# The offset of the first layer norm: from a negated mean on VectorE and a product on GpSimd to one more VectorE instruction behind the inverse root

## Chip, cores and metric

One core of one Trainium2 chip runs the kernel. The metric is the device time of one execution in microseconds (us); lower is better. Engines are written PE (TensorE), DVE (VectorE), ACT (ScalarE), POOL (GpSimd) and SP (SyncE, which issues DMAs here).

## What is computed

Two graph layers on 128 graphs of 128 nodes with 128 features, each with a residual and a layer norm. With this adjacency (0 or 1, ones on the diagonal) the 39 relations of the first layer that need values from 2 to 40 are empty, and so are three of the four relations of the second.

```python
def _layernorm(x, axis=-1, eps=1e-05):
    m = jnp.mean(x, axis=axis, keepdims=True)
    v = jnp.var(x, axis=axis, keepdims=True)
    return (x - m) / jnp.sqrt(v + eps)
...
h = x @ W.T
g = h @ Wg.T
vals = (h[:, :, None, :] + b) * jax.nn.sigmoid(g[:, :, None, :] + bg)
...
x = _layernorm(x + relu(adj_t @ vals))            # first layer, in short
x = _layernorm(x + (adj == 1) @ x @ weight + bias)  # second layer, in short
```

## The kernel before

The 128 graphs are taken in 32 groups of 4 (`GROUPS`, `GB`), a tile being 128 partitions (nodes) by 512 (4 graphs by 128 features), all fp32. The group number is q, and each engine has its own program, written as a loop over iterations t in which it works on several groups at different stages. Nothing but that written order and semaphores orders the work.

In iteration t, PE projects group t (`hg_ps`, L379), sums the neighbours of group t-1 (`loop_ps`, L391), multiplies the messages of group t-5 by their weights (`y_ps`, L430) and gathers the messages of group t-3 (`msg_ps`, L409). ACT makes the gate of group t (L524), seeds the next bank (L515), copies messages (L534), writes normalised output (L551) and looks at the adjacency (L560).

DVE does in iteration t, in this order: the second sum `z_sb` of group t-5 (L753) and its two halves of statistics (L757), the gated values of group t (L727), the first sum `s_sb` of group t-1 (L735) and its statistics (L742). Between these stand the nine steps of one inverse root per iteration, the chain (`inverse_root`, L665, L668, L671, L676, L679, L682, L685, L688, L691), on tiles of 128 by 8: four graphs of the first norm and four of the second. Every step reads the one before it and waits for it by the semaphore `chain_done`. The ninth writes `rstd`. In iterations 2 to 4, before the first `z_sb` exists, all nine steps run in one piece ahead of the values (L727); from iteration 5 on they are woven between the large instructions, and the ninth stands right before the next `z_sb`.

The first norm is x1 = s * rstd + nmr with nmr = -mean * rstd. Its means are read with the statistics: `negative_means` writes `mean_neg` (L710, 128 by 4), called between the third and fourth step of the chain. POOL waits for `chain_done` and `mean_done`, multiplies to `nmr` (L320, 128 by 4), waits for that product, and makes x1 in four instructions, one a graph (L328). It then issues one adjacency DMA (L303 or L310). PE's messages of that group wait for `x1_done`, and DVE's own `z_sb` and the reuse of the rings do too. The last group's product is made by DVE (`last_norm1`, L790), and its x1 is shared by POOL, DVE and ACT.

Of the kernel before, what the change touches and what calls it, by code (L numbers as in the profile page):

```python
# [59 lines left out]
def build(nc, x, x_t, adj, adj_t, w_in, w_loop_t, wg_loop_t, gate_bias, w_msg, msg_bias,  # L60
          w_rel_t, wg_rel_t, b_rel, bg_rel, w_msgs, rel_ids, identity, out):
    with ExitStack() as ctx:
        def sb(name, shape, dt):
            return ctx.enter_context(nc.sbuf_tensor(name, shape, dt))
# [20 lines left out]
        stats = sb("stats", [P, STATS_RING, 4, 6], F32)  # L85
        rstd = sb("rstd", [P, RSTD_RING, 2, GB], F32)
        nmr = sb("nmr", [P, 2, GB], F32)
        mean_neg = sb("mean_neg", [P, 2, GB], F32)
        tiny = sb("tiny", [P, 2, 6, 2 * GB], F32)
        last_stats = sb("last_stats", [P, 2, 4, 6], F32)  # L90
        last_rstd = sb("last_rstd", [P, 2, 2 * GB], F32)
# [71 lines left out]
        bn2_done = sem("bn2_done")  # L163
        chain_done = [sem(f"chain_done{j}") for j in range(2)]
        last_done = [sem(f"last_done{j}") for j in range(2)]
        mean_done = sem("mean_done")
        nmr_done = sem("nmr_done")
        last_nmr = sem("last_nmr")
        last_bn = sem("last_bn")
        x1_act = sem("x1_act")  # L170
        x1_dve = sem("x1_dve")
# [124 lines left out]
        @block.gpsimd  # L296
        def _(pool):
            def load_adj(k):
                if 0 <= k < PAIRS:
                    spot = k % ADJ_RING  # L300
                    await_count(pool, loop_done, 2 * (k - ADJ_RING) + 2)
                    await_count(pool, seen_done, 2 * (k - ADJ_RING) + 2)
                    pool.dma_start(adj_sb[:, 2 * spot:2 * spot + 2, :].rearrange("p g n -> p (g n)"), adj[k])\  # L303
                        .then_inc(adj_in[spot], 16)

            def load_adjt(k):
                if 0 <= k < PAIRS:
                    spot = k % ADJ_RING
                    await_count(pool, msg_done, 2 * (k - ADJ_RING) + 2)
                    pool.dma_start(adjt_sb[:, 2 * spot:2 * spot + 2, :].rearrange("p g n -> p (g n)"), adj_t[k])\  # L310
                        .then_inc(adjt_in[spot], 16)

            def norm1(q):
                if exists(q):
                    t = q + NORM1_LAG
                    pool.wait_ge(chain_done[t % 2], chain_end(t))
                    r, n = rstd[:, t % RSTD_RING, 0, :], nmr[:, t % 2, :]
                    if q < GROUPS - 1:
                        pool.wait_ge(mean_done, q + 1)
                        nc.gpsimd.tensor_tensor(n, mean_neg[:, t % 2, :], r, ALU.mult).then_inc(nmr_done, 1)  # L320
                        pool.wait_ge(nmr_done, q + 1)
                    else:
                        pool.wait_ge(last_nmr, 1)

                    await_count(pool, msg_done, q - X1_RING + 1)
                    await_count(pool, z_done, q - X1_RING + 1)
                    for b in range(GB) if q < GROUPS - 1 else (2,):
                        last = nc.gpsimd.tensor_scalar(  # L328
                            x1[:, q % X1_RING, batch(b)], s_sb[:, q % S_RING, batch(b)],
                            r[:, b:b + 1], n[:, b:b + 1], ALU.mult, ALU.add)  # L330
                    last.then_inc(x1_done, 1)


            pool.wait_ge(fold_in, 16 * 2)
            load_adj(0)
            load_adj(1)
            load_adjt(0)
            load_adj(2)
            load_adjt(1)
            for t in range(GROUPS + NORM1_LAG):  # L340
                norm1(t - NORM1_LAG)
                if t % 2 == 0:
                    load_adj(t // 2 + 3)
                else:
                    load_adjt(t // 2 + 2)

            def general_pair(pair):
                pool.dma_start(adj_sb[:, 0:2, :], adj[bass.ds(pair, 1)].rearrange("o p (g n) -> p (o g) n", g=2))\
                    .then_inc(gadj_in, 16)
                pool.dma_start(adjt_sb[:, 0:2, :], adj_t[bass.ds(pair, 1)].rearrange("o p (g n) -> p (o g) n", g=2))\  # L350
                    .then_inc(gadj_in, 16)
                pool.wait_ge(gout_ready, pair * 2 + 2)

            general(pool, general_pair)
# [145 lines left out]
        def _(act):  # L500
# [76 lines left out]
            copy_messages(GROUPS - 3)  # L577
            norm2(GROUPS - 6, every)
            copy_messages(GROUPS - 2)
            act.wait_ge(last_nmr, 1)  # L580
            t = GROUPS - 1 + NORM1_LAG
            nc.scalar.activation(x1[:, (GROUPS - 1) % X1_RING, batch(3)], s_sb[:, (GROUPS - 1) % S_RING, batch(3)],
                                 ACT.Identity, bias=nmr[:, t % 2, 3:4],
# [43 lines left out]
        def _(dve):  # L627
# [32 lines left out]
                dve.wait_ge(w1_mid, 4)  # L660
                tt(w1[:, :], b1_mid[:, :], aux_ps[:, P:2 * P], ALU.subtract).then_inc(w1_mid, 2)

            def inverse_root(m2, r, done, before, work, aside=None):
                var, y0, y1, yy, a, w = (work[:, i, :] for i in range(6))
                ts(var, m2, 1.0 / P, EPS, ALU.mult, ALU.add).then_inc(done, 1)  # L665
                yield
                dve.wait_ge(done, before + 1)
                ts(y0.bitcast(I32), var.bitcast(I32), -0.5, GUESS, ALU.mult, ALU.add).then_inc(done, 1)  # L668
                yield
                dve.wait_ge(done, before + 2)  # L670
                tt(yy, y0, y0, ALU.mult).then_inc(done, 1)  # L671
                yield
                if aside is not None:
                    aside()
                dve.wait_ge(done, before + 3)
                tt(a, yy, var, ALU.mult).then_inc(done, 1)  # L676
                yield
                dve.wait_ge(done, before + 4)
                stt(w, a, CUBIC1, a, ALU.add, ALU.mult).then_inc(done, 1)  # L679
                yield  # L680
                dve.wait_ge(done, before + 5)
                stt(y1, w, CUBIC0, y0, ALU.add, ALU.mult).then_inc(done, 1)  # L682
                yield
                dve.wait_ge(done, before + 6)
                tt(yy, y1, y1, ALU.mult).then_inc(done, 1)  # L685
                yield
                dve.wait_ge(done, before + 7)
                stt(w, yy, -0.5, var, ALU.mult, ALU.mult).then_inc(done, 1)  # L688
                yield
                dve.wait_ge(done, before + 8)  # L690
                stt(r, w, 1.5, y1, ALU.add, ALU.mult).then_inc(done, 1)  # L691

            def chain(t):

                if FIRST_CHAIN <= t <= LAST_CHAIN:
                    await_count(dve, bn1_done, t - NORM1_LAG + 1)
                    await_count(dve, bn2_done, t - STAT2_LAG + 1)

                    await_count(dve, x1_done, t - RSTD_RING - NORM1_LAG + 1)
                    await_count(dve, out_done, t - RSTD_RING - STAT2_LAG + 1)  # L700
                    before = chain_end(t) - CHAIN_OPS
                    await_count(dve, chain_done[t % 2], before)
                    m2 = stats[:, t % STATS_RING, :, :].rearrange("p c (i k) -> p (c i) k", k=3)[:, :, 2]
                    r = rstd[:, t % RSTD_RING, :, :].rearrange("p l b -> p (l b)")

                    def negative_means():

                        await_count(dve, x1_done, t - 2 - NORM1_LAG + 1)
                        means = stats[:, t % STATS_RING, 0:2, :].rearrange("p c (i k) -> p (c i) k", k=3)[:, :, 1]
                        ts(mean_neg[:, t % 2, :], means, -1.0, None, ALU.mult).then_inc(mean_done, 1)  # L710

                    yield from inverse_root(m2, r, chain_done[t % 2], before, tiny[:, t % 2, :, :], negative_means)

            def last_chain(k):

# [67 lines left out]
            def last_norm1(q):  # L783
                t = q + NORM1_LAG
                r, n = rstd[:, t % RSTD_RING, 0, :], nmr[:, t % 2, :]
                dve.wait_ge(chain_done[t % 2], chain_end(t))

                dve.wait_ge(x1_done, q - 1)
                dve.wait_ge(mean_done, q + 1)
                tt(n, mean_neg[:, t % 2, :], r, ALU.mult).then_inc(last_nmr, 1)  # L790
                dve.wait_ge(last_nmr, 1)

                dve.wait_ge(msg_done, q - X1_RING + 1)
                dve.wait_ge(z_done, q - X1_RING + 1)
                for b in range(2):
                    last = ts(x1[:, q % X1_RING, batch(b)], s_sb[:, q % S_RING, batch(b)], r[:, b:b + 1], n[:, b:b + 1],
                              ALU.mult, ALU.add)
                last.then_inc(x1_dve, 1)
# [7 lines left out]
            for t in range(GROUPS + 1):  # L806
# [6 lines left out]
                if exists(t - Z_LAG):  # L813
                    second_sum(t - Z_LAG)
                    step(1)
                    second_stats(t - Z_LAG, 0)
                    step(1)
                    second_stats(t - Z_LAG, 1)
                    step(2)
                else:  # L820
                    step(CHAIN_OPS)
                if exists(t):
                    values(t)
                if t == 1:
# [4 lines left out]
                if exists(t - LOOP_LAG):  # L829
# [2 lines left out]
                    first_stats(t - LOOP_LAG, 0)  # L832
                    step(1)
                    first_stats(t - LOOP_LAG, 1)
                step(CHAIN_OPS)
            for _ in chain(LAST_CHAIN):
                pass
            last_norm1(GROUPS - 1)
# [136 lines left out]
```

## Time and profile before

| what | value |
|---|---|
| time, median of 3 runs | 169.39 us (169.31 to 169.51) |
| the profiled execution: its time, and its span | 168.68 us, 166.9 us |
| TensorE clock granted, mean | 0.985 |
| busy, share of the span | PE 91%, DVE 88%, ACT 75%, POOL 47% |
| chain that ended last | PE 78%, DMA 8%, DVE 7% |

The span runs from the first to the last instruction; the execution's time is 1.78 us longer than its span. Busy time counts an instruction from its start to its end. On DVE consecutive instructions overlap in the trace by 0.06 to 0.09 us, so what one costs is read from the distance between starts and not from its duration.

### The profile page before, as it was taken

What the parts mean: (1) busy time and instruction counts of PE and PEld (TensorE: products, weight loads), DVE (VectorE), ACT (ScalarE), POOL (GpSimd) and SP (SyncE); (2) the same over time, 40 slices, a digit from 0 to 9 for tenths busy, and PEclk for the clock granted to TensorE, in tenths of its full rate; (3) what the DMA queues carried; (4) which work ended last, traced back from release to release, by engine and by line L of the source; (5) the groups of instructions that cost most, each with busy time, mean ns of one, the idle gap of its engine ahead of it and who ended that gap; (6) DMA issues with size and microseconds to landing.
All of it is one profiled execution on the core that took longest, in us unless ns stands there. A gap on an engine that the chain in (4) does not pass through costs nothing.

```text
span 166.9 us, 3913 instructions
## 1 busy us (share of the span) xinstructions
PE 151.6 (91%) x1072; PEld 140.4 (84%) x1072; DVE 146.7 (88%) x583; ACT 126.0 (75%) x287; POOL 78.6 (47%) x192
## 2 busy tenths in 40 slices
PE   6864899999999999999999999999999999998920
PEld 2553689999999999999999999999999999997910
DVE  1225999999999999999999999999999999999771
ACT  3266455679888888888888889998888888844661
POOL 2700366155555555565555555555554544446000
PEclk9999999999999999999999999999999999999985
DMA  4999999965999999999999899999995341131133
GB/s 137 342 389 394 397 401 403 308 196 189 298 302 306 310 304 274 280 312 301 268 305 329 272 277 333 325 310 298 253 324 212 85 166 63 65 130 63 64 125 138
DMA packets 19465, 42.76 MB, mean 256 GB/s; under 512 B 2160, under 2 KB 3056, under 8 KB 19440
## 3 DMA queue, kind: packets, MB, share of 16 engines
q1 hardware_dynamic: 13968, 25.24, 44.0%
q0 software_dynamic: 4608, 16.78, 33.2%
q10 hardware_dynamic: 864, 0.46, 0.9%
q8 instruction: 10, 0.16, 0.4%
q14 instruction: 15, 0.12, 0.3%
HBM read 34.08 MB, written 8.39 MB: 254 GB/s over the span
## 4 chain that ended last, share of the span: by engine, by line
PE 78%; DMA 8%; DVE 7%; issue 3%; ACT 1%; ACTq 0%; DVEq 0%
PE hg_ps L379 28%; PE msg_ps L409 16%; PE y_ps L430 15%; PE loop_ps L391 15%; DMA b<-msg_bias_dram 5%; DMA gate_b<-gate_bias_dram 2%; PE hg_ps L430 2%; PE hg_ps L426 2%; DVE s_sb L735 2%; DVE stats L742 1%; PE y_ps L426 1%; PE hg_ps L409 1%; ACT out_sb L551 1%; DVE z_sb L753 0%; DVE tiny L679 0%
## 5 line engine op out<-in xcount | busy, mean ns | idle before, releaser
L379 PE MATMUL hg_ps<-w_gate,xt_sb 128*128 128x256 f32 x256 | 60.8, 380 | 2.6 <-ACT hg_ps L515 2.5
L328 POOL TENSOR_SCALAR x<-s_sb,rstd,nmr 128x128 f32<-128x128 f32 x125 | 54.7, 446 | 3.7 <-DVE rstd L691 0.4
L379 PEld LDWEIGHTS hg_ps<-w_gate,xt_sb 128*128 128x128 f32 x256 | 46.2, 190 | 8.5 <-issue 3.0
L320 POOL TENSOR_TENSOR nmr<-mean_neg,rstd 128x4 f32<-128x4 f32 x31 | 6.0, 194 | 68.8 <-DVE rstd L691 68.8
L551 ACT ACTIVATE out_sb<-z_sb,rstd 128x128 f32<-128x128 f32 x112 | 38.0, 391 | 0.2 <-DVE rstd L691 0.2
L391 PEld LDWEIGHTS loop_ps<-vals,adj_sb 128*128 128x128 f32 x256 | 33.3, 191 | 5.2 <-issue 3.8
L391 PE MATMUL loop_ps<-vals,adj_sb 128*128 128x128 f32 x256 | 34.0, 276 | 2.6 <-DVE s_sb L735 2.6
L524 ACT ACTIVATE gate<-hg_ps 128x512 f32<-128x512 f32 x32 | 19.1, 597 | 22.2 <-PE hg_ps L379 22.1
L515 ACT ACTIVATE hg_ps<-gate_b 128x1024 f32<-128x1024 f32 (+1 forms) x32 | 32.3, 1010 | 1.0 <-DMA gate_b<-gate_bias_dram 1.0
L409 PE MATMUL msg_ps<-adjt_sb,x 128*128 128x128 f32 x248 | 33.0, 276 | 0.0
L430 PE MATMUL y_ps<-w,msg_t 128*128 128x128 f32 x232 | 30.6, 275 | 0.0
L409 PEld LDWEIGHTS msg_ps<-adjt_sb,x 128*128 128x128 f32 x248 | 30.2, 192 | 0.2 <-issue 0.2
L430 PEld LDWEIGHTS y_ps<-w,msg_t 128*128 128x128 f32 x232 | 28.2, 192 | 0.0
L727 DVE TENSOR_TENSOR vals<-hg_ps,gate 128x512 f32<-128x512 f32 x32 | 22.0, 688 | 6.4 <-ACT gate L524 5.7
L742 DVE BATCH_NORM_STATS2 stats<-s_sb 128x6 f32<-128x256 f32 x64 | 26.5, 426 | 0.3
L757 DVE BATCH_NORM_STATS2 stats<-z_sb 128x6 f32<-128x256 f32 x56 | 23.7, 427 | 0.0
L560 ACT ACTIVATE seen<-adj_sb,half 128x512 bf16<-128x512 f32 x32 | 22.7, 710 | 1.3 <-DMA adj_sb<-adj_dram 1.3
L534 ACT ACTIVATE msg_t<-msg_ps 128x512 f32<-128x512 f32 x31 | 18.0, 581 | 6.6 <-PE msg_ps L409 6.6
L735 DVE SCALAR_TENSOR_TENSOR s_sb<-loop_ps,x_sb 128x512 f32<-128x512 f32 x32 | 21.8, 682 | 0.0
L753 DVE TENSOR_TENSOR z_sb<-y_ps,x 128x512 f32<-128x512 f32 x28 | 19.1, 682 | 0.0
L303 POOL DMA_DIRECT2D adj_sb<-adj_dram x16 | 9.6, 598 | 2.8 <-DMA wg_t<-wg_loop_t_dram 2.8
L310 POOL DMA_DIRECT2D adjt_sb<-adj_t_dram x16 | 9.5, 591 | 0.0
(66 smaller groups left out, 104.9 us busy)
## 6 DMA issues: line engine op xcount, KB each, us to landing
xt_sb<-x_t_dram SPq DMA_DIRECT2D x32, 256.0 KB, 4.9
x_sb<-x_dram SPq DMA_DIRECT2D x32, 256.0 KB, 5.0
adj_sb<-adj_dram POOLq DMA_DIRECT2D x16, 512.0 KB, 5.5
adjt_sb<-adj_t_dram POOLq DMA_DIRECT2D x16, 512.0 KB, 5.2
out<-out_sb SPq DMA_DIRECT2D x32, 256.0 KB, 4.1
gate_b<-gate_bias_dram ACTq DMA_DIRECT2D x1, 128.0 KB, 3.4
w_loop<-w_loop_dram ACTq DMA_DIRECT2D x1, 64.0 KB, 2.0
wg_t<-wg_loop_t_dram SPq DMA_DIRECT2D x1, 64.0 KB, 2.2
```

What stands on the lines that cost most here:

```text
L328: last = nc.gpsimd.tensor_scalar(x1[:, q % X1_RING, batch(b)], s_sb[:, q % S_RING, batch(b)], r[:, b:b + 1], n[:, b:b + 1], ALU.mult, ALU.add)
L379: last = nc.tensor.matmul(hg_ps[:, q % 2, b, :], xt_sb[:, q % XT_RING, batch(b)], w_gate[:, :], start=False, stop=True, skip_group_check=True)
L391: last = nc.tensor.matmul(loop_ps[:, batch(b)], adj_sb[:, spot, batch(b)], vals[:, q % 2, batch(b)], start=True, stop=True)
L409: last = nc.tensor.matmul(msg_of(q)[:, batch(b)], x1[:, q % X1_RING, batch(b)], adjt_sb[:, spot, batch(b)], start=True, stop=True)
L430: last = nc.tensor.matmul(y_of(q)[:, batch(b)], msg_t[:, q % 2, batch(b)], w1[:, :], start=q < LAST, stop=True, skip_group_check=q >= LAST)
L515: nc.scalar.activation(hg_ps[:, q % 2, 0:graphs, :], gate_b[:, None, :].broadcast_to([P, graphs, 2 * P]), ACT.Copy).then_inc(seeded, 1)
L551: last = nc.scalar.activation(out_sb[:, q % OUT_RING, batch(b)], src, ACT.Copy, scale=r)
L560: nc.scalar.activation(seen[:, :], adj_sb[:, 2 * spot + q % 2, :], ACT.Square, bias=half[:, 0:1], accum_out=seen_sum[:, q:q + 1]).then_inc ...
L727: tt(vals[:, q % 2, :].rearrange("p (b n) -> p b n", b=GB), hg_ps[:, q % 2, :, 0:P], gate[:, q % 2, :].rearrange("p (b n) -> p b n", b=GB) ...
L735: stt(s_sb[:, q % S_RING, :], loop_ps[:, :], 0.0, x_sb[:, q % X_RING, :], ALU.max, ALU.add)\
L742: got = nc.vector.bn_stats(stats[:, (q + NORM1_LAG) % STATS_RING, p, :], s_sb[:, q % S_RING, 2 * p * P:2 * (p + 1) * P].rearrange("p (i n) ...
L757: got = nc.vector.bn_stats(stats[:, (q + STAT2_LAG) % STATS_RING, 2 + p, :], z_sb[:, q % Z_RING, 2 * p * P:2 * (p + 1) * P].rearrange("p ( ...
```

## The change

The negated means are gone, with their tile, the product on POOL and the one in `last_norm1`. Behind the ninth step DVE waits for it and writes `nmr` itself in one instruction, (mean * -1) * rstd, from the statistics and `rstd`; the semaphore `nmr_done` now carries it to POOL, ACT and DVE. The places at which the program lets "all remaining" steps run now take ten.

```diff
             def norm1(q):
                 if exists(q):
                     t = q + NORM1_LAG
-                    pool.wait_ge(chain_done[t % 2], chain_end(t))
                     r, n = rstd[:, t % RSTD_RING, 0, :], nmr[:, t % 2, :]
-                    if q < GROUPS - 1:
-                        pool.wait_ge(mean_done, q + 1)
-                        nc.gpsimd.tensor_tensor(n, mean_neg[:, t % 2, :], r, ALU.mult).then_inc(nmr_done, 1)
-                        pool.wait_ge(nmr_done, q + 1)
-                    else:
-                        pool.wait_ge(last_nmr, 1)
+
+                    pool.wait_ge(nmr_done, q + 1)
...
-                    def negative_means():
-
-                        await_count(dve, x1_done, t - 2 - NORM1_LAG + 1)
-                        means = stats[:, t % STATS_RING, 0:2, :].rearrange("p c (i k) -> p (c i) k", k=3)[:, :, 1]
-                        ts(mean_neg[:, t % 2, :], means, -1.0, None, ALU.mult).then_inc(mean_done, 1)
-
-                    yield from inverse_root(m2, r, chain_done[t % 2], before, tiny[:, t % 2, :, :], negative_means)
+                    yield from inverse_root(m2, r, chain_done[t % 2], before, tiny[:, t % 2, :, :])
+                    yield
+                    dve.wait_ge(chain_done[t % 2], before + CHAIN_OPS)
+
+                    await_count(dve, x1_done, t - 2 - NORM1_LAG + 1)
+                    means = stats[:, t % STATS_RING, 0:2, :].rearrange("p c (i k) -> p (c i) k", k=3)[:, :, 1]
+                    stt(nmr[:, t % 2, :], means, -1.0, rstd[:, t % RSTD_RING, 0, :], ALU.mult, ALU.mult)\
+                        .then_inc(nmr_done, 1)
...
             def last_norm1(q):
                 t = q + NORM1_LAG
                 r, n = rstd[:, t % RSTD_RING, 0, :], nmr[:, t % 2, :]
-                dve.wait_ge(chain_done[t % 2], chain_end(t))
-
-                dve.wait_ge(x1_done, q - 1)
-                dve.wait_ge(mean_done, q + 1)
-                tt(n, mean_neg[:, t % 2, :], r, ALU.mult).then_inc(last_nmr, 1)
-                dve.wait_ge(last_nmr, 1)
+                dve.wait_ge(nmr_done, q + 1)
```

On DVE the first place is the first chain, iteration 2, which ends ahead of `vals`. Before:

```order
L671 TENSOR_TENSOR tiny<-tiny 128x8
L710 TENSOR_SCALAR mean_neg<-stats 128x4
L676 TENSOR_TENSOR tiny<-tiny 128x8
L679 SCALAR_TENSOR_TENSOR tiny<-tiny 128x8
L682 SCALAR_TENSOR_TENSOR tiny<-tiny 128x8
L685 TENSOR_TENSOR tiny<-tiny 128x8
L688 SCALAR_TENSOR_TENSOR tiny<-tiny 128x8
L691 SCALAR_TENSOR_TENSOR rstd<-tiny 128x8
L727 TENSOR_TENSOR vals<-hg_ps,gate 128x512
```

And the same place on DVE with the change (its line numbers are those of the changed file, 8 to 10 lower):

```order
L663 TENSOR_TENSOR tiny<-tiny 128x8
L666 TENSOR_TENSOR tiny<-tiny 128x8
L669 SCALAR_TENSOR_TENSOR tiny<-tiny 128x8
L672 SCALAR_TENSOR_TENSOR tiny<-tiny 128x8
L675 TENSOR_TENSOR tiny<-tiny 128x8
L678 SCALAR_TENSOR_TENSOR tiny<-tiny 128x8
L681 SCALAR_TENSOR_TENSOR rstd<-tiny 128x8
L702 SCALAR_TENSOR_TENSOR nmr<-stats,rstd 128x4
L718 TENSOR_TENSOR vals<-hg_ps,gate 128x512
```

The filler between two dependent steps has gone, and a dependent instruction stands at the end, ahead of the values. On DVE the second place is the turn from one iteration to the next once the chain is woven in (from iteration 5). Before:

```order
L742 BN_STATS stats<-s_sb 128x6
L691 SCALAR_TENSOR_TENSOR rstd<-tiny 128x8
L753 TENSOR_TENSOR z_sb<-y_ps,x 128x512
L665 TENSOR_SCALAR tiny<-stats 128x8
L757 BN_STATS stats<-z_sb 128x6
L668 TENSOR_SCALAR tiny<-tiny 128x8
L757 BN_STATS stats<-z_sb 128x6
L671 TENSOR_TENSOR tiny<-tiny 128x8
L710 TENSOR_SCALAR mean_neg<-stats 128x4
L676 TENSOR_TENSOR tiny<-tiny 128x8
L727 TENSOR_TENSOR vals<-hg_ps,gate 128x512
```

With the change, on DVE at the same place:

```order
L733 BN_STATS stats<-s_sb 128x6
L681 SCALAR_TENSOR_TENSOR rstd<-tiny 128x8
L702 SCALAR_TENSOR_TENSOR nmr<-stats,rstd 128x4
L744 TENSOR_TENSOR z_sb<-y_ps,x 128x512
L657 TENSOR_SCALAR tiny<-stats 128x8
L748 BN_STATS stats<-z_sb 128x6
L660 TENSOR_SCALAR tiny<-tiny 128x8
L748 BN_STATS stats<-z_sb 128x6
L663 TENSOR_TENSOR tiny<-tiny 128x8
L666 TENSOR_TENSOR tiny<-tiny 128x8
L718 TENSOR_TENSOR vals<-hg_ps,gate 128x512
```

The new instruction stands between the ninth step and `z_sb`, with nothing between it and the step that it reads. On POOL one iteration before, with its waits in brackets:

```order
L320 TENSOR_TENSOR nmr<-mean_neg,rstd 128x4 [waits mean_done,chain_done0]
L328 TENSOR_SCALAR x<-s_sb,rstd,nmr 128x128 [waits z_done,msg_done,nmr_done]
L328 TENSOR_SCALAR x<-s_sb,rstd,nmr 128x128 x3
L303 DMA adj_sb<-adj_dram 128x1024 [waits seen_done,loop_done]
```

And on POOL with the change:

```order
L320 TENSOR_SCALAR x<-s_sb,rstd,nmr 128x128 [waits z_done,msg_done,nmr_done]
L320 TENSOR_SCALAR x<-s_sb,rstd,nmr 128x128 x3
L300 DMA adj_sb<-adj_dram 128x1024 [waits seen_done,loop_done]
```

POOL's first instruction of a group is now x1 itself (the changed file's L320 is the old L328).

## Rows read from the trace of the kernel before

**Rows 1.** The chain that ended last, shares of the span by engine.

```profile
PE 78%; DMA 8%; DVE 7%; issue 3%; ACT 1%; ACTq 0%; DVEq 0%
```

**Rows 2.** 58 to 145 us: length; busy PE, PEld, DVE, ACT, POOL; clock; DMA.

```profile
58.00:145.00 87.00, 87.00 (x632) 82.87 (x631) 85.56 (x338) 76.75 (x180) 47.51 (x116) 1.00 0.83 258
```

**Rows 3.** Timeline of one iteration, 81 to 85.5 us: start us, us, what.

```profile
81.01 0.68 DVE L753 TENSOR_TENSOR z_sb<-y_ps,x 128x512 f32<-128x512 f32 x1
81.18 0.19 POOL L320 TENSOR_TENSOR nmr<-mean_neg,rstd 128x4 f32<-128x4 f32 x1 [1.82 <-DVE rstd L691]
...
81.48 1.73 POOL L328 TENSOR_SCALAR x<-s_sb,rstd,nmr 128x128 f32<-128x128 f32 x4
81.61 0.15 DVE L665 TENSOR_SCALAR tiny<-stats 128x8 f32<-128x8 f32 x1
...
82.07 0.31 DVE L668 TENSOR_SCALAR tiny<-tiny 128x8 int32<-128x8 int32 x1
...
82.41 0.60 ACT L524 ACTIVATE gate<-hg_ps 128x512 f32<-128x512 f32 x1 [0.52 <-PE hg_ps L379]
82.63 0.17 DVE L671 TENSOR_TENSOR tiny<-tiny 128x8 f32<-128x8 f32 x1
82.72 0.15 DVE L710 TENSOR_SCALAR mean_neg<-stats 128x4 f32<-128x4 f32 x1
82.83 0.21 DVE L676 TENSOR_TENSOR tiny<-tiny 128x8 f32<-128x8 f32 x1
...
83.03 0.69 DVE L727 TENSOR_TENSOR vals<-hg_ps,gate 128x512 f32<-128x512 f32 x1
...
83.99 1.06 PE L409 MATMUL msg_ps<-adjt_sb,x 128*128 128x128 f32 x8
84.32 0.15 DVE L682 SCALAR_TENSOR_TENSOR tiny<-tiny 128x8 f32<-128x8 f32 x1
...
84.50 0.17 DVE L685 TENSOR_TENSOR tiny<-tiny 128x8 f32<-128x8 f32 x1
...
85.34 0.15 DVE L691 SCALAR_TENSOR_TENSOR rstd<-tiny 128x8 f32<-128x8 f32 x1
85.41 0.69 DVE L753 TENSOR_TENSOR z_sb<-y_ps,x 128x512 f32<-128x512 f32 x1
```

**Rows 4.** Timelines of DVE and of POOL in an early iteration.

```profile
33.10 0.68 DVE L753 TENSOR_TENSOR z_sb<-y_ps,x 128x512 f32<-128x512 f32 x1
...
34.17 0.15 DVE L668 TENSOR_SCALAR tiny<-tiny 128x8 int32<-128x8 int32 x1
...
34.66 0.28 DVE L710 TENSOR_SCALAR mean_neg<-stats 128x4 f32<-128x4 f32 x1
...
37.28 0.68 DVE L753 TENSOR_TENSOR z_sb<-y_ps,x 128x512 f32<-128x512 f32 x1
...
33.58 1.76 POOL L328 TENSOR_SCALAR x<-s_sb,rstd,nmr 128x128 f32<-128x128 f32 x4
```

**Rows 5.** Timeline of PE at the start of the loop.

```profile
20.56 1.13 PE L391 MATMUL loop_ps<-vals,adj_sb 128*128 128x128 f32 x8 [0.74 <-DVE s_sb L735]
...
35.44 0.79 PE L409 MATMUL msg_ps<-adjt_sb,x 128*128 128x128 f32 x5
```

**Rows 6.** Timeline of the end of the loop, 147 to 154 us.

```profile
147.03 0.15 DVE L691 SCALAR_TENSOR_TENSOR rstd<-tiny 128x8 f32<-128x8 f32 x1
...
150.90 0.15 DVE L691 SCALAR_TENSOR_TENSOR rstd<-tiny 128x8 f32<-128x8 f32 x1
...
151.44 1.84 POOL L328 TENSOR_SCALAR x<-s_sb,rstd,nmr 128x128 f32<-128x128 f32 x4
...
151.63 0.31 DVE L676 TENSOR_TENSOR tiny<-tiny 128x8 f32<-128x8 f32 x1
...
152.90 0.40 DVE L691 SCALAR_TENSOR_TENSOR rstd<-tiny 128x8 f32<-128x8 f32 x1
...
153.39 1.13 PE L409 MATMUL hg_ps<-adjt_sb,x 128*128 128x128 f32 x8 [0.76 <-issue]
```

More of the change, by code:

```diff
@@ L87, in build @@
         nmr = sb("nmr", [P, 2, GB], F32)
-        mean_neg = sb("mean_neg", [P, 2, GB], F32)
         tiny = sb("tiny", [P, 2, 6, 2 * GB], F32)
@@ L165, in build @@
         last_done = [sem(f"last_done{j}") for j in range(2)]
-        mean_done = sem("mean_done")
         nmr_done = sem("nmr_done")
-        last_nmr = sem("last_nmr")
         last_bn = sem("last_bn")
@@ L579, in _ @@
             copy_messages(GROUPS - 2)
-            act.wait_ge(last_nmr, 1)
+            act.wait_ge(nmr_done, GROUPS)
             t = GROUPS - 1 + NORM1_LAG
@@ L661, in message_weight_end, with inverse_root @@
                 tt(w1[:, :], b1_mid[:, :], aux_ps[:, P:2 * P], ALU.subtract).then_inc(w1_mid, 2)
-            def inverse_root(m2, r, done, before, work, aside=None):
+            def inverse_root(m2, r, done, before, work):
                 var, y0, y1, yy, a, w = (work[:, i, :] for i in range(6))
@@ L672, in inverse_root @@
                 yield
-                if aside is not None:
-                    aside()
                 dve.wait_ge(done, before + 3)
@@ L820, in _ @@
                 else:
-                    step(CHAIN_OPS)
+                    step(CHAIN_OPS + 1)
                 if exists(t):
@@ L834, in _ @@
                     first_stats(t - LOOP_LAG, 1)
-                step(CHAIN_OPS)
+                step(CHAIN_OPS + 1)
             for _ in chain(LAST_CHAIN):
```

## The prediction

> **What bounds the kernel now.** I read the chain that ended last first: PE holds 78% of it [rows 1]. The busy time by stretch then shows a PE without a gap from 58 to 145 us (87.00 of 87.00 us), but also a DVE that is busy for 85.56 of them [rows 2]. So PE sets the pace, and DVE runs right beside it; the question is how much room DVE has, and only the timeline of one iteration tells.
>
> One iteration takes 85.41 - 81.01 = 4.40 us, z_sb to z_sb [rows 3]. DVE has one real wait in it: the gate ends at 82.41 + 0.60 = 83.01, and `vals` starts at 83.03. Without that wait `vals` would follow L676 some 0.09 us before that one's end (83.04), at 82.95. DVE's room is 0.08 us an iteration, its own pace 4.32. In the early iteration of [rows 4] it ran at 37.28 - 33.10 = 4.18. The difference has a cause that matters below: L668 took 0.31 us in the one and 0.15 in the other.
>
> **A small instruction beside POOL.** POOL's x1 is four instructions of 0.43 to 0.44 us each. L668 at 82.07 starts 0.16 us into the second (81.48 + 0.43 = 81.91), takes 0.31 and ends 0.47 behind that one's start. At 34.17 it is 0.15 us into the second (33.58 + 0.44) and takes 0.15. L710 at 34.66 starts 0.20 into the third and takes 0.28; L710 at 82.72 starts 0.37 into one and takes 0.15; L676 at 151.63 starts 0.19 into the first (151.44), takes 0.31 and ends 0.50 behind its start [rows 3, 4, 6]. So a small DVE instruction that starts between about 0.16 and 0.3 us into a POOL instruction is held until that ends, and one that starts earlier or later goes through.
>
> **The change part by part.**
>
> Removed on DVE: L710. L671 starts at 82.63 and L676, which waits for it, at 82.83: 0.20. L682 to L685, dependent too and with nothing between, is 0.18 [rows 3]. L710 stood in the shadow of that wait, so its removal returns 0, at most 0.02. Removed on POOL: L320 with its wait. From the start of L691 to x1 it is 81.48 - 81.01 + 0.07 = 0.54 (L691 starts 0.07 ahead of z_sb, 85.34 to 85.41).
>
> Added on DVE: `nmr` behind L691, which it reads. Before, L691 to the next instruction was 0.07 [rows 3]. Now L691 to `nmr` is a dependent distance, 0.18 to 0.20 (I take 0.19), and `nmr` to the next 0.08: 0.27, so +0.20 us an iteration. The trace has no such instruction of 128 by 4 with three operands; the dependent steps of 128 by 8 at 0.17 are the nearest rows. Bounds: +0.01, if it had a plain place in line (0.08), and +0.20 as said. The dependence is written in the code, so I take +0.20. POOL gets `nmr` at 0.19 + 0.17 and starts 0.10 later (L691's end, 81.01 - 0.07 + 0.15 = 81.09, to L320 at 81.18 was 0.09): x1 starts 0.46 to 0.47 behind L691, 0.07 earlier than before.
>
> The start. In iterations 2 to 4 the chain stands in one piece ahead of `vals` and `s_sb`, and PE waits for `s_sb` (0.74 us at 20.56 [rows 5]). Each of the three chains puts DVE back by 0.20, hence 0.60 by iteration 5. There POOL's x1 for group 3 ends at 33.58 + 1.76 = 35.34 [rows 4], and PE's messages start at 35.44, 0.1 behind it [rows 5]: this hand-over decides. Shift of PE from here: 0.60 - 0.07 = **+0.53 us**. There is no cover for it, since PE has no gap behind it.
>
> The even part. Where do DVE's small steps fall against POOL now? Counting from the start of z_sb, POOL's first x1 starts at 0.46 - 0.27 = 0.19 and its fourth at 0.19 + 1.30 = 1.49. L668 (at 1.06) starts 0.01 into the third, so its stretch of 0.16 goes. L671 comes at 1.62 - 0.16 = 1.46, and L676 at 1.66: 0.17 to 0.18 into the fourth. By the rows above it is held until 0.47 to 0.50 behind that one's start, 1.96 to 1.99, and `vals` could start at 1.87 to 1.90. From `vals` to the next z_sb it is 85.41 - 83.03 = 2.38, and +0.20 for `nmr`. DVE's own pace becomes 4.45 to 4.48 us; with 0.02 on the distances, 4.42 to 4.48. I take **4.45**, which is above PE's 4.40. Then DVE no longer catches up after the start and sets the pace: x1 arrives later each time, and PE waits at its messages. In the even part x1 was ready at 81.48 + 1.73 = 83.21 and wanted at 83.99 [rows 3], but the start uses this slack up.
>
> The end. PE waits 0.76 us at 153.39 for x1 of group 30, which POOL ended at 151.44 + 1.84 = 153.28 [rows 6]; behind it PE runs without DVE's help until the last statistics. So the shift of that x1 is the shift of the whole. From L691 of iteration 5 (33.10 - 0.06 = 33.04) to that of iteration 32 (150.90) it was 117.86 us. Now it is 26 x 4.45, and a last period without `vals` of about 4.0 (150.90 - 147.03 = 3.87 before, +0.20 for `nmr`, -0.16 for L668, +0.10 for L676): 119.7, or +1.84.
>
> Sum: 0.53 + 1.84 = **+2.4 us**, 171.1 against this execution's 168.68. The median of runs is 0.71 above that execution, so 169.39 + 2.4 = **171.8 us**. With 4.42 or 4.48 in place of 4.45 it is 0.8 less or more: 171.0 to 172.6.
>
> **A rule that makes it worse.** The trace lets an instruction through that starts up to 0.15 us into a POOL instruction: L665 at 81.61 is 0.13 into the first and takes 0.15 [rows 3]. If such an early start were held as well, L668, now 0.01 into the third, would be held to 0.19 + 0.87 + 0.47 = 1.53 in place of 1.21: L671 would come at 1.78, L676 at 1.98 when POOL is through, `vals` at 2.06, and the pace would be 2.06 + 2.38 + 0.20 = 4.64. The Trainium skill (SBUF — State Buffer, Who interferes with whom) has this rule: VectorE and GpSimd lock a shared port pair for a whole instruction, and the later one is fully blocked. By that rule the trace agrees for starts from 0.16 us on and disagrees for L665.
>
> **The rivals.**
>
> (a) PE stays the bound. If L676 slips through, `vals` could start at 1.66 + 0.09 = 1.75, and the pace is 1.75 + 2.38 + 0.20 = 4.33, under 4.40. Then only the start remains, and the end (+0.20 for `nmr`, -0.16 for L668, -0.07 on POOL) is -0.03: +0.5 us, 169.9. It decides at L676's start, 0.15 or 0.16 into the fourth; I have 0.17 to 0.18. For it speaks that the distance to the edge is 0.02 us; against it, that L691 at 152.90 took 0.40 beside a fourth instruction [rows 6], and that L676 at 82.83 took 0.21 when hardly 0.06 into one.
>
> (b) The early start is held too, pace 4.64: 0.53 + 117.86 replaced by 26 x 4.64 + 4.3 = 124.9, so +7.6: 177.0. Against it speaks L665.
>
> (c) Not slower. `nmr` takes a place without a wait, at +0.01 in place of +0.20: then the start costs 0.03 and gives 0.07 on POOL, and the last period loses L668's 0.16 and POOL's 0.07, in all about -0.25 us: 169.1. This needs the dependent distance to fall under about 0.09 us; nothing in the trace does, all are 0.18 or more.
>
> **How the numbers follow.** DVE sets the pace (4.42 to 4.48): 0.65. (a) 0.22. (b) 0.04. (c) 0.04. The remaining 0.05 lies between the main case and (a), a pace near 4.40 that works the lag off slowly. A change of this kernel can be told from none at about 0.2%, 0.34 us. The likeliest is 171.8 with its own range of 171.0 to 172.6. The range that holds 8 in 10 reaches to (a) and leaves (b) and (c) out: 169.8 to 172.7. Slower holds the main case, (b), what lies between, and most of (a) (+0.5 against 0.34): 0.85; same the rest of (a) and part of (c): 0.11; faster 0.04.
>
> **What the changed profile would show.** In every iteration `nmr` starts 0.19 us behind the ninth step, and the next instruction 0.08 behind `nmr`; x1 starts on POOL 0.46 behind the ninth step. PE's messages at 35.44 come near 35.97. In the even part z_sb to z_sb is 4.45 and not 4.40, the fourth step takes about 0.3 us, L668 0.15, `vals` starts clear of the gate's end, and PE shows small waits at the messages. The prediction is wrong if the fourth step takes 0.15 to 0.21 us and the period is 4.40: then (a) holds.

## The result, and the profile after

The changed kernel takes 171.37 us (median of 4 runs, 170.90 to 172.08) beside 169.45 us for the kernel before (169.31 to 169.56): the ratio is 1.0116, with a 95% interval of 1.0091 to 1.0142. It is 1.9 us slower; 171.8 was forecast, and 171.0 to 172.6 as the likeliest case's own range. Between the two profiled executions (168.68 and 171.13 us) the difference is 2.45 us.

Three lines of the changed kernel's page, and its busy time by stretch from 58 to 145 us (columns as in [rows 2]):

```profile
span 169.3 us, 3878 instructions
...
DVE 54%; issue 27%; DMA 8%; PE 6%; DVEq 1%; ACT 1%; ACTq 0%
...
L666 DVE TENSOR_TENSOR tiny<-tiny 128x8 f32<-128x8 f32 x34 | 7.5, 219 | 1.2
```

```profile
58.00:145.00 87.00, 86.96 (x628) 82.72 (x627) 84.68 (x333) 76.11 (x177) 42.24 (x94) 1.00 0.83 263
```

The chain that ended last has gone from PE (78% in [rows 1]) to DVE, with 54%, and PE's share is 6%. "Issue" (27%) is time between the DVE instructions of that chain for which the profile shows no releaser. The busy times do not tell this at all: PE is busy for 86.96 of 87.00 us as before, and DVE, which now sets the pace, is busy for less than before (84.68 against 85.56 us), because the second step is no longer held and the fourth step and `nmr` stand behind short idle times, 0.04 and 0.03 us (84.69 to 84.73 and 82.91 to 82.94 below). L666, the old L676, is the fourth step of the chain.

One iteration of the changed kernel, timeline from 82.7 to 87.5 us:

```profile
82.76 0.15 DVE L681 SCALAR_TENSOR_TENSOR rstd<-tiny 128x8 f32<-128x8 f32 x1
...
82.94 0.16 DVE L702 SCALAR_TENSOR_TENSOR nmr<-stats,rstd 128x4 f32<-128x4 f32 x1
...
83.05 0.69 DVE L744 TENSOR_TENSOR z_sb<-y_ps,x 128x512 f32<-128x512 f32 x1
...
83.22 1.73 POOL L320 TENSOR_SCALAR x<-s_sb,rstd,nmr 128x128 f32<-128x128 f32 x4 [2.16 <-DVE nmr L702]
...
83.55 0.58 ACT L516 ACTIVATE gate<-hg_ps 128x512 f32<-128x512 f32 x1
...
84.13 0.15 DVE L660 TENSOR_SCALAR tiny<-tiny 128x8 int32<-128x8 int32 x1
...
84.53 0.16 DVE L663 TENSOR_TENSOR tiny<-tiny 128x8 f32<-128x8 f32 x1
84.73 0.23 DVE L666 TENSOR_TENSOR tiny<-tiny 128x8 f32<-128x8 f32 x1
84.89 0.68 DVE L718 TENSOR_TENSOR vals<-hg_ps,gate 128x512 f32<-128x512 f32 x1
...
87.48 0.69 DVE L744 TENSOR_TENSOR z_sb<-y_ps,x 128x512 f32<-128x512 f32 x1
```

z_sb to z_sb is 87.48 - 83.05 = 4.43 us (4.40 in [rows 3]). `vals` starts 0.76 us behind the gate's end (83.55 + 0.58 = 84.13) where before it waited for it. `nmr` starts 0.18 behind the ninth step, and z_sb 0.11 behind `nmr`, 0.29 in all where 0.07 was: +0.22. The second step (L660) takes 0.15 and is no longer held. The fourth step starts 0.22 us into POOL's fourth x1 instruction (84.51 to 84.95 in the trace), takes 0.23, and `vals` follows 0.16 behind its start and not 0.08.

Counted from z_sb's start, `vals` now starts at 1.84 us (84.89 - 83.05). In the kernel before it could start at 1.94 (82.95 by the prediction's estimate, less 81.01). So the insertion adds 0.22 us, and the steps ahead of `vals` give back about 0.1: the second step's hold is gone (-0.16), a new one stands at the fourth. That is how DVE's own pace comes from 4.32 to 4.43 us and not to 4.54.

Start and end of the changed kernel, from its timelines of PE, DVE and POOL:

```profile
16.16 0.68 DVE L726 SCALAR_TENSOR_TENSOR s_sb<-loop_ps,x_sb 128x512 f32<-128x512 f32 x1
...
21.00 1.13 PE L383 MATMUL loop_ps<-vals,adj_sb 128*128 128x128 f32 x8 [0.93 <-DVE s_sb L726]
...
21.45 0.59 POOL L300 DMA_DIRECT2D adj_sb<-adj_dram  x1
...
21.69 0.31 DVE L657 TENSOR_SCALAR tiny<-stats 128x8 f32<-128x8 f32 x1
...
25.36 1.13 PE L383 MATMUL loop_ps<-vals,adj_sb 128*128 128x128 f32 x8 [0.60 <-DVE s_sb L726]
...
33.98 0.15 DVE L681 SCALAR_TENSOR_TENSOR rstd<-tiny 128x8 f32<-128x8 f32 x1
...
34.44 1.73 POOL L320 TENSOR_SCALAR x<-s_sb,rstd,nmr 128x128 f32<-128x128 f32 x4 [4.04 <-DVE nmr L702]
...
36.27 0.91 PE L401 MATMUL msg_ps<-adjt_sb,x 128*128 128x128 f32 x6
...
118.83 0.69 DVE L744 TENSOR_TENSOR z_sb<-y_ps,x 128x512 f32<-128x512 f32 x1 [0.30 <-issue]
...
149.44 0.15 DVE L681 SCALAR_TENSOR_TENSOR rstd<-tiny 128x8 f32<-128x8 f32 x1
...
153.41 0.15 DVE L681 SCALAR_TENSOR_TENSOR rstd<-tiny 128x8 f32<-128x8 f32 x1
...
155.69 1.13 PE L401 MATMUL hg_ps<-adjt_sb,x 128*128 128x128 f32 x8 [0.43 <-issue]
```

PE waits longer for `s_sb` (0.93 us against 0.74 in [rows 5]), the messages of iteration 6 start at 36.27 (35.44), the ninth step of iteration 32 at 153.41 (150.90), and group 30's messages at 155.69 (153.39 in [rows 6]): 2.3 us later. Of that, 0.25 us is not the change's: the first s_sb of this execution starts at 16.16 and that of the kernel before at 15.91, behind a DMA of the message bias that ended at 14.61 and 14.35. The first s_sb of the kernel before, timeline of DVE:

```profile
15.91 0.68 DVE L735 SCALAR_TENSOR_TENSOR s_sb<-loop_ps,x_sb 128x512 f32<-128x512 f32 x1
```

### The profile page after: what moved, and what is told of

The parts are those of the page before. It is cut to its first block, busy times and chain, and to the rows that moved or that the text cites. A ratio compares the mean times of both kernels' runs of the same rounds, so it can differ in the third digit from the quotient of the medians.

```text
span 169.3 us, 3878 instructions
## 1 busy us (share of the span) xinstructions
PE 152.9 (90%) x1072; PEld 141.2 (83%) x1072; DVE 147.3 (87%) x582; ACT 125.8 (74%) x287; POOL 71.6 (42%) x161
## 4 chain that ended last, share of the span: by engine, by line
DVE 54%; issue 27%; DMA 8%; PE 6%; DVEq 1%; ACT 1%; ACTq 0%
DVE stats L748 11%; DVE s_sb L726 11%; DMA b<-msg_bias_dram 6%; DVE stats L733 5%; DVE tiny L657 3%; DVE vals L718 3%; DVE rstd L681 3%; DVE tiny L669 3%; DVE tiny L678 3%; DVE z_sb L744 2%; DMA gate_b<-gate_bias_dram 2%; DVE tiny L663 2%; DVE tiny L672 2%; PE hg_ps L422 2%; DVE tiny L660 2%
## 5 line engine op out<-in xcount | busy, mean ns | idle before, releaser
L320 POOL TENSOR_SCALAR x<-s_sb,rstd,nmr 128x128 f32<-128x128 f32 x125 | 54.3, 441 | 82.0 <-DVE nmr L702 82.0
L401 PE MATMUL msg_ps<-adjt_sb,x 128*128 128x128 f32 x248 | 33.5, 278 | 0.1
L516 ACT ACTIVATE gate<-hg_ps 128x512 f32<-128x512 f32 x32 | 18.6, 580 | 10.1 <-PE hg_ps L371 10.1
L666 DVE TENSOR_TENSOR tiny<-tiny 128x8 f32<-128x8 f32 x34 | 7.5, 219 | 1.2
```

The lines of the kernel that those rows point to most:

```text
L320: last = nc.gpsimd.tensor_scalar(x1[:, q % X1_RING, batch(b)], s_sb[:, q % S_RING, batch(b)], r[:, b:b + 1], n[:, b:b + 1], ALU.mult, ALU.add)
L401: last = nc.tensor.matmul(msg_of(q)[:, batch(b)], x1[:, q % X1_RING, batch(b)], adjt_sb[:, spot, batch(b)], start=True, stop=True)
```

## The experiments

They ran in three groups (E1 to E4, E5 to E8, E9 to E12), each on a chip of its own, the ratio each time to the kernel before on that chip (medians 168.7 to 168.9 us). There its runs spread over more than 1%, so the intervals are wider. Much of the spread lies ahead of the loop: in the profiled executions the first s_sb starts anywhere between 15.24 and 16.68 us. So where traces are compared below, times are counted from it. "The old way" is the negated mean on DVE and the product on POOL.

### Where it costs: the start and the loop apart

E1 is the kernel before with `nmr` on DVE in the first three chains alone; E2 is the changed kernel with the old way there, and E6 is E2 again, beside E5, the changed kernel again.

```diff
+OLD = 3
...
-                    pool.wait_ge(nmr_done, q + 1)
+                    if q < OLD:
+                        pool.wait_ge(chain_done[t % 2], chain_end(t))
+                        pool.wait_ge(mean_done, q + 1)
+                        nc.gpsimd.tensor_tensor(n, mean_neg[:, t % 2, :], r, ALU.mult).then_inc(nmr_old, 1)
+                        pool.wait_ge(nmr_old, q + 1)
+                    else:
+                        pool.wait_ge(nmr_done, q + 1 - OLD)
```

> The kernel before, with the new way (nmr on VectorE behind the ninth step) in the first three chains alone, iterations 2 to 4. Theory (two causes, start and pace): the three insertions put VectorE and so the x1 of group 3 back by 3 x 0.20 = 0.60 us, and from there the old loop runs at PE's 4.40 with VectorE catching up; total +0.6 us, 170.05, and PE's messages of iteration 6 start near 36.04 in place of 35.44. Rival (only the pace of the even part costs): no change, 169.4.

> The changed kernel, with the old way (negated means and a product on GpSimd) in the first three chains alone. Theory: VectorE's pace in the even part stays 4.43 us and sets the time from the first woven iteration on, but all of it begins 0.60 us earlier: 171.37 - 0.6 = 170.8. Rival (only the pace costs): 171.4, as the changed kernel.

> The changed kernel once more, on the same chip as the three beside it, as their base. Theory: 1.012 of before, with VectorE's pace 4.43 us between rare longer iterations.

> The changed kernel with the old way in the first three chains, once more beside the changed kernel on the same chip. In the first run it came out 1.010 of before, too near to the changed kernel's 1.012 to say whether the start adds to the pace. Theory (start and pace add up, since VectorE sets the time from the first woven iteration on): 0.6 us under the changed kernel, 1.008. Rival (they do not add up): 1.012.

E1 gave 1.0037 (1.0012 to 1.0061): 0.6 us from three chains out of 32, as the theory said. In its trace the messages of iteration 6 start 0.68 us later than in the kernel before (35.81 - 15.60 against 35.44 - 15.91). E2 gave 1.0102 (1.0064 to 1.0140), too wide to tell; side by side E5 gave 1.0148 (1.0104 to 1.0192) and E6 1.0107 (1.0076 to 1.0138), 0.7 us apart in the ratios' middles with intervals that still overlap. In the traces E6's first z_sb starts 0.68 us earlier than E5's and its last z_sb 0.45 us earlier. So start and loop both cost; that only the pace costs is refuted by E1. That the start's 0.6 to 0.7 us adds to the loop's in full is likely but not shown.

### One more instruction, or where the fourth step falls

E3 moves the fourth step one instruction later. E4 adds an instruction that nobody reads to the kernel before.

```diff
 # e3, on the changed kernel
                     second_stats(t - Z_LAG, 1)
-                    step(2)
+                    step(1)
...
-                step(1)
+                step(2)
                 if exists(t - LOOP_LAG):
```

```diff
 # e4, on the kernel before
                     yield from inverse_root(m2, r, chain_done[t % 2], before, tiny[:, t % 2, :, :], negative_means)
+                    yield
+                    dve.wait_ge(chain_done[t % 2], before + CHAIN_OPS)
+                    await_count(dve, spare_done, t - FIRST_CHAIN - 1)
...
+                    stt(spare[:, t % 2, :], means, -1.0, rstd[:, t % RSTD_RING, 0, :], ALU.mult, ALU.mult)\
+                        .then_inc(spare_done, 1)
```

> The changed kernel with the chain's fourth step moved behind the gated values from iteration 5 on: same instructions, same number, but the fourth step no longer starts inside POOL's fourth x1 instruction and no longer right behind the third step. Theory (the hold by POOL lifts VectorE's pace over PE's): the turn third step to first sum goes from 1.03 to 0.94 us, pace 4.34 on its own, under PE's 4.40, so that z_sb to z_sb is 4.40, vals waits for the gate again, and only the start's 0.5 us is left: 169.95. Rival (one more instruction on VectorE is what costs, wherever it stands): 171.4.

> The kernel before with one more instruction: behind the ninth step, and waiting for it, the same three-operand instruction as the change has, but written to a tile that nobody reads; the negated means and POOL's product stay. VectorE has one instruction more than in the changed kernel. Theory (a small instruction costs by where it falls against POOL): POOL's x1 starts 0.27 behind z_sb's start in place of 0.47, L668 falls between two of its instructions and is not held, the fourth step starts 0.09 into the fourth; pace 4.37 on its own, PE's 4.40 holds, and the start costs 0.6: 170.05. Rival (the added 0.20 adds to the pace of 4.32 wherever it falls): 4.52, 26 x 0.12 + 1.2 = +4.3 us, 173.7.

Both missed; the theory had E3 0.5 us and E4 0.6 us over the kernel before. E3 gave 1.0098 (1.0065 to 1.0131), 1.8 us slower. Timeline of DVE in E3:

```profile
82.55 0.69 DVE L744 TENSOR_TENSOR z_sb<-y_ps,x 128x512 f32<-128x512 f32 x1
...
84.12 0.68 DVE L718 TENSOR_TENSOR vals<-hg_ps,gate 128x512 f32<-128x512 f32 x1
84.72 0.15 DVE L666 TENSOR_TENSOR tiny<-tiny 128x8 f32<-128x8 f32 x1
84.91 0.17 DVE L669 SCALAR_TENSOR_TENSOR tiny<-tiny 128x8 f32<-128x8 f32 x1
85.02 0.69 DVE L726 SCALAR_TENSOR_TENSOR s_sb<-loop_ps,x_sb 128x512 f32<-128x512 f32 x1
...
86.94 0.69 DVE L744 TENSOR_TENSOR z_sb<-y_ps,x 128x512 f32<-128x512 f32 x1
```

The fourth step is not held (0.15), and the chain that ended last is PE's again at 78%. But the pace is 4.39 and not the 4.34 of my expectation: a large instruction starts 0.11 behind a short step that itself had to wait (84.91 to 85.02), where I had counted 0.07 to 0.08. At 4.39 against 4.40 hardly anything of the start's lag is worked off: `vals` is still 0.38 us behind the gate in the last iteration (0.03 in the kernel before), a long iteration of 4.74 us included, and at the end of the loop PE waits 0.71 us for `z_sb`, where it waited 0.20 before. So a chain that shows 78% PE does not mean that DVE costs nothing.

E4 gave 1.0252 (1.0205 to 1.0298), 4.2 us slower, near the rival's 4.3 and not the theory's 0.6. Its timeline of DVE, z_sb and the fourth step (here L678):

```profile
79.31 0.69 DVE L761 TENSOR_TENSOR z_sb<-y_ps,x 128x512 f32<-128x512 f32 x1
80.98 0.38 DVE L678 TENSOR_TENSOR tiny<-tiny 128x8 f32<-128x8 f32 x1
83.88 0.69 DVE L761 TENSOR_TENSOR z_sb<-y_ps,x 128x512 f32<-128x512 f32 x1
85.54 0.20 DVE L678 TENSOR_TENSOR tiny<-tiny 128x8 f32<-128x8 f32 x1
88.24 0.69 DVE L761 TENSOR_TENSOR z_sb<-y_ps,x 128x512 f32<-128x512 f32 x1
...
92.81 0.69 DVE L761 TENSOR_TENSOR z_sb<-y_ps,x 128x512 f32<-128x512 f32 x1
94.47 0.17 DVE L678 TENSOR_TENSOR tiny<-tiny 128x8 f32<-128x8 f32 x1
97.15 0.69 DVE L761 TENSOR_TENSOR z_sb<-y_ps,x 128x512 f32<-128x512 f32 x1
```

Here the same instruction, in the same place of the program, takes 0.38 us in some iterations and 0.17 to 0.20 in others. With 0.38 the period is 83.88 - 79.31 = 4.57; with 0.20 it is 88.24 - 83.88 = 4.36, with 0.17 it is 97.15 - 92.81 = 4.34. The inserted instruction is in all of them. So the insertion leaves a pace under PE's 4.40 where no step is held (the second step is not in E4 either: it takes 0.15), and the hold by POOL takes it over; the rival's reason, 0.20 added wherever it falls, would give 4.52 in every iteration. My error was to let a start 0.09 us into POOL's instruction pass: of the 22 that started 0.08 to 0.11 in, 18 took 0.38, of the five at 0.12 and 0.13 none.

### nmr behind the next large instruction

E7 takes `nmr` out of the chain and issues it behind z_sb, E8 does so only from the ninth chain on, with the old way before.

```diff
             def offset(t):
                 if FIRST_CHAIN <= t <= LAST_CHAIN:
                     dve.wait_ge(chain_done[t % 2], chain_end(t))
...
                 if exists(t - Z_LAG):
                     second_sum(t - Z_LAG)
+                    if t > Z_LAG:
+                        offset(t - 1)
                     step(1)
```

> The changed kernel with nmr one place later: behind z_sb (behind the values in the first three chains), so that a large instruction covers its wait for the ninth step; at the very end, where nothing stands between, right behind the ninth step. Theory: the instruction then costs 0.08 and not 0.29 us, VectorE's own pace is 4.25, PE's 4.40 holds and vals waits for the gate; but x1 starts 0.87 behind z_sb's start in place of 0.17, and in the start PE waits for the x1 of group 3: +0.6 us there, 1.0035 of before. Rival (x1's delay of 0.7 us is what PE sees in every iteration, the slack of 0.68 being used up): slower than the changed kernel, 1.02.

> Old way in the first eight chains, then nmr behind z_sb as in e7. Theory: the start is that of the kernel before, PE's 4.40 holds in the even part, and only the end differs: L668 no longer held and no product on POOL ahead of group 30's x1, 0.1 to 0.15 us less; 0.9995 of before, no difference that can be told. Rival (an instruction more on VectorE or the later x1 costs in the even part): 1.01.

E7 gave 1.0096 (1.0064 to 1.0128), E8 1.0047 (1.0018 to 1.0076); both came out slower than the theory had them (1.0035 and 0.9995). Timelines of DVE and POOL in E7:

```profile
83.30 0.69 DVE L746 TENSOR_TENSOR z_sb<-y_ps,x 128x512 f32<-128x512 f32 x1
83.91 0.16 DVE L704 SCALAR_TENSOR_TENSOR nmr<-stats,rstd 128x4 f32<-128x4 f32 x1
...
84.39 0.25 DVE L660 TENSOR_SCALAR tiny<-tiny 128x8 int32<-128x8 int32 x1
...
85.10 0.39 DVE L666 TENSOR_TENSOR tiny<-tiny 128x8 f32<-128x8 f32 x1
85.42 0.68 DVE L720 TENSOR_TENSOR vals<-hg_ps,gate 128x512 f32<-128x512 f32 x1
...
87.78 0.69 DVE L746 TENSOR_TENSOR z_sb<-y_ps,x 128x512 f32<-128x512 f32 x1
...
84.18 1.73 POOL L320 TENSOR_SCALAR x<-s_sb,rstd,nmr 128x128 f32<-128x128 f32 x4 [2.21 <-DVE nmr L704]
```

`nmr` costs 0.07 here (83.91 to the next step at 83.97), as expected. But POOL now starts 0.88 behind z_sb, and two steps run into it: the second 0.21 us into POOL's first instruction (0.25), the fourth 0.06 into its third (0.39). The period is 4.48 us, longer than the changed kernel's, although the insertion is cheaper. E8 has the same 0.39 and 4.48 in its loop; the rival of E8, a cost of the later x1, was not yet excluded.

### The hold taken away

The next four put one tile of the chain, the square `yy` that the third step writes and the fourth reads, into PSUM from iteration 5 on. Nothing else changes: same instructions, same order. The third step then writes PSUM, and the fourth has one operand in SBUF and not two. The seventh and eighth steps use the same tile for the second square, so they change in the same way.

```diff
-            def inverse_root(m2, r, done, before, work):
+            def inverse_root(m2, r, done, before, work, squares=None):
                 var, y0, y1, yy, a, w = (work[:, i, :] for i in range(6))
+                if squares is not None:
+                    yy = aux_ps[:, squares:squares + 2 * GB]
...
+                    squares = 3 * P + t % 2 * 2 * GB if t >= Z_LAG else None
```

> The changed kernel, with the tile between the third and the fourth step (the square yy, 128 by 8) in PSUM from iteration 5 on and in SBUF before: same instructions in the same places, but the fourth step now reads only one operand from SBUF. Theory (POOL's fourth x1 instruction holds the fourth step, since both read SBUF): the fourth step takes 0.17 and not 0.23 us, VectorE's own pace is 4.36 and not 4.43 us, PE's 4.40 sets the pace again, and the lag is worked off: 1.004 of before, from the start and the end. Rival (what costs is the inserted instruction and its wait alone, the fourth step's 0.23 is its own): 1.012 to 1.015, period 4.43. Second rival (PSUM's slower access takes what the hold gave): the same, with a third-to-fourth distance over 0.20.

> As e9, with the old way in the first three chains. Theory: the start's 0.6 us goes as well: 1.001 to 1.002 of before, that is the changed loop costs nothing that can be told once the start and the hold are taken out. Rival (the insertion alone): 1.008 to 1.011 as e6.

> e8 (old way in eight chains, then nmr behind z_sb) with the square in PSUM. In e8 the fourth step started 0.06 us into POOL's third x1 instruction and took 0.39; the period was 4.47. Theory: it takes 0.17, the period is PE's 4.40 with vals waiting for the gate, 0.9995 of before. Rival (the later x1 costs): period over 4.40, 1.005 as e8.

> The kernel before with the same square in PSUM, as a control of PSUM itself. Theory: PE's 4.40 holds as it did; no difference that can be told, 1.000 +- 0.002. If PSUM's access were slower by more than 0.08 us a chain, VectorE would pass 4.40 and this would be slower.

| run | without PSUM | with `yy` in PSUM |
|---|---|---|
| changed kernel | E5: 1.0148 (1.0104 to 1.0192) | E9: 1.0049 (1.0021 to 1.0077) |
| changed, old start | E6: 1.0107 (1.0076 to 1.0138) | E10: 1.0014 (0.9985 to 1.0043) |
| nmr behind z_sb, late | E8: 1.0047 (1.0018 to 1.0076) | E11: 1.0018 (0.9991 to 1.0045) |
| kernel before | 1 | E12: 1.0000 (0.9980 to 1.0019) |

E9's fourth step (L668 there: shortest, median and longest in ns, over the 29 chains with PSUM), and an iteration of it:

```profile
L668 DVE TENSOR_TENSOR tiny<-aux_ps,tiny x29: 166/166/168, 30.9 to 152.3; 128x8 f32<-128x8 f32 x29
```

```profile
83.19 0.17 DVE L665 TENSOR_TENSOR aux_ps<-tiny 128x8 f32<-128x8 f32 x1
83.39 0.17 DVE L668 TENSOR_TENSOR tiny<-aux_ps,tiny 128x8 f32<-128x8 f32 x1
83.48 0.69 DVE L721 TENSOR_TENSOR vals<-hg_ps,gate 128x512 f32<-128x512 f32 x1
...
81.88 1.74 POOL L320 TENSOR_SCALAR x<-s_sb,rstd,nmr 128x128 f32<-128x128 f32 x4 [2.11 <-DVE nmr L705]
```

It starts 0.23 us into POOL's fourth instruction (at 83.17 in the trace), where the changed kernel's was held, and takes 0.17 every time; the distance to the third step stays 0.20, so PSUM costs nothing there. (E12 agrees, but a cost under DVE's 0.08 us of room would not show in it.) The intervals of E5 and E9, and of E6 and E10, do not meet; those of E8 and E11 do. E9's pace is 4.36 to 4.37, and the lag of `vals` behind the gate shrinks from 1.05 us to 0.04 in iteration 24; a long iteration of 4.72 us throws it back to 0.33, and 0.09 is left in the last. The chain that ended last is PE's again, with 68%. In E10 the insertion is still in 29 of the 32 chains, and no difference is left that can be told from none; its interval reaches to +0.4%, and in its trace `vals` is still 0.21 us behind the gate in the last iteration.

Two operands in SBUF are not the whole condition of a hold: the second step reads one tile alone and is held too, for 0.31 us in [rows 3] and for 0.25 in E11.

E11 is E8, where the fourth step was held longest, with `yy` in PSUM. Its timeline of DVE:

```profile
85.29 0.68 DVE L768 TENSOR_TENSOR z_sb<-y_ps,x 128x512 f32<-128x512 f32 x1
87.09 0.17 DVE L679 TENSOR_TENSOR tiny<-aux_ps,tiny 128x8 f32<-128x8 f32 x1
87.32 0.69 DVE L742 TENSOR_TENSOR vals<-hg_ps,gate 128x512 f32<-128x512 f32 x1
...
89.69 0.69 DVE L768 TENSOR_TENSOR z_sb<-y_ps,x 128x512 f32<-128x512 f32 x1
```

0.17 in place of 0.39, and z_sb to z_sb is 4.40 with `vals` waiting for the gate (0.03 us behind its end from iteration 8 on). PE is busy for 87.00 of the 87.00 us from 58 to 145. The later x1 therefore costs nothing in the loop, although the chain that ended last now runs over it, as E11's page has it:

```profile
POOL 30%; issue 30%; DVE 20%; DMA 7%; PE 7%; ACT 1%; DVEq 0%; POOLq 0%; ACTq 0%
```

None of the versions beats the kernel before: PE's 4.40 us an iteration bounds them all from below.

## Why the prediction was right

- **What bounds.** Right: DVE's room was 0.08 us an iteration, and the change took more. PE's chain of 78% became DVE's of 54%.
- **The removed L710 returns nothing.** Right: third to fourth step is 0.20 us before and after. POOL's part too: x1 starts 0.46 behind the ninth step (82.76 to 83.22).
- **The insertion, +0.20.** 0.22: the 0.18 to `nmr` was right (0.19 was taken), but z_sb stands 0.11 and not 0.08 behind it.
- **The start, +0.53.** Against the first s_sb of each execution, the ninth step of iteration 5 starts 0.69 us later and not 0.60, and x1 of group 3 0.61 us later (34.44 - 16.16 = 18.28 against 33.58 - 15.91 = 17.67). The term lacked 0.14 us that DVE's first step of iteration 3 lost (0.04 came back at the second step of iteration 4): L657 takes 0.31 beside POOL's DMA issue of 21.45, a neighbour that the old timing avoided. E1 has the same 0.31 beside its issue. That it was the DMA issue is read from this coincidence alone.
- **The pace, 4.45.** 4.43. The hold came at the forecast place, POOL's fourth instruction, but the step starts 0.22 us into it and not 0.17 to 0.18, and it ended 0.45 to 0.46 behind that one's start and not 0.47 to 0.50: 0.23 us and not about 0.3. The rule behind it, held from about 0.16 us on and not before, is too simple (last section).
- **The stretch from iteration 5 to 32, +1.84.** (153.41 - 33.98) - 117.86 = +1.57, of which 0.35 is one long iteration at 118.83 that my term did not have. The last period was 3.97 (4.0). Without the long iteration the term would be +1.22, so it was 0.6 us too large (0.02 us in each of 26 periods, and rounding), and luck gave more than half of that back.
- **The sum, +2.4.** 1.9 between the medians, whose interval reaches from 1.5 to 2.4. The 2.45 between the profiled executions looks exact and is partly luck too: 0.25 of it came ahead of the first s_sb. The mechanism was right, and its size in the loop was overestimated.
- **Rival (a)**, PE stays the bound, did not hold for the change. It describes E9 and E10, where the hold is gone; with its 4.33 it was 0.03 too fast, so the lag is worked off more slowly than it says. **Rival (b)**, the early start held too, did not occur: L660 starts 0.04 into an instruction and takes 0.15. By that rule of the Trainium skill (SBUF — State Buffer, Who interferes with whom) the second step would have been blocked; the part that E9 tests, that the fourth step contends with two SBUF inputs and does not with one, agrees with the trace (0.23 against 0.17). **Rival (c)** failed on the distance, 0.29.

## What to carry over

When a second engine runs within a tenth of a microsecond of the one that bounds, price an inserted instruction by the distance between starts, dependence included, and then place every small instruction of the period anew against its neighbours on GpSimd: here the insertion (0.22) moved one step off its hold (0.16 back) and would have stayed under PE's pace in the loop, and the new hold of another step (0.07) took it over. At the start, where nothing hides DVE, the three insertions cost 0.6 us with or without a hold (E1). What the hold would cost alone was not run. A cheaper insertion (E7) can be slower in the loop, for it moves GpSimd under other steps. A lag of the start is only hidden if the loop has room to work it off, and moving one operand to PSUM (E9, 1.0049) gave more here than moving the instruction (E3, 1.0098), though the two ran on different chips and their intervals touch.

## What was not expected

- The length of a hold is set by when POOL's instruction ends, 0.44 to 0.47 us behind its start; whether there is one is not set by the start alone. The second step of the kernel before starts 0.15 to 0.17 us into POOL's second instruction in all 27 iterations: in 20 it takes 0.30 to 0.32, in the other seven 0.15 to 0.16, and in those POOL's instruction takes 0.46 to 0.47 in place of 0.44. [rows 3] and [rows 4] show one of each, so the edge at 0.16 us that the prediction read from them is not one. Steps that started 0.06 us in, after waiting for the step before, took 0.39 in 23 iterations of E7 and 0.17 in four, and in those four POOL's instruction took 0.48 in place of 0.44: one of the two waits. Steps queued behind a longer instruction were never held when they started up to 0.14 us in. What decides between is open.
- A large instruction with three waits starts 0.11 us behind a short one that itself had waited, and 0.07 to 0.08 behind others. In the first three iterations in which `z_sb` follows `nmr`, where it has two waits and not three, it starts 0.08 behind.
- Long iterations (0.35 us at 118.83, marked as issue) stand at the same instruction in E3, E5 and E9, and in E2, E6 and E10, which share the old start, at another, near 50 us. The other runs have none of this length. The kernel before has stretches of 0.14 us more on DVE, and its PE hides them. What they are was not tried, and up to 0.35 of the change's 1.9 us may be theirs.
